# Quantised ffn of a two-layer decoder: GpSimd adds two tiles back ahead of the row quantisation, TensorE and ScalarE in another order, six unread 512-column products a tile

## The chip, the core and the metric

The kernel runs on one NeuronCore of a Trainium2 chip, in one launch. The metric is the device time of the launch in microseconds (us). The core has five engines that run their own instruction lists and meet at semaphores: TensorE (PE, matrix products into PSUM), VectorE (DVE), ScalarE (ACT), GpSimd (POOL, SBUF only) and SyncE (SP, here the DMA queue). Each takes its instructions strictly in order; an instruction whose semaphore isn't there yet holds up all that stand behind it on the same engine.

## The reference

A pre-norm decoder of two layers on x of 64 x 64 rows of 256 numbers: attention, cross attention and an ffn, each added to x, twice. Only the last ffn is touched. It quantises its inputs, its weights and its hidden rows to whole numbers from -127 to 127 with one scale a row:

```python
def _quant_dequant(v, axis):
    scale = jnp.max(jnp.abs(v), axis=axis, keepdims=True) / QMAX   # QMAX = 127
    scale = jnp.maximum(scale, EPS)
    q = jnp.clip(jnp.round(v / scale), -QMAX, QMAX)
    return q * scale

xq = _ste(x, axis=-1)                    # x: the layer-normed rows, 256 wide
gate_up = jnp.einsum('bsh,oh->bso', xq, _ste(w_gate_up, axis=-1))
gate, up = (gate_up[..., :I], gate_up[..., I:])          # I = 704
h = jax.nn.silu(gate) * up
return jnp.einsum('bsi,oi->bso', _ste(h, axis=-1), _ste(w_down, axis=-1))
# and the decoder: x = x + _L1_ffn_ref(_layernorm(x), ...)
```

`_ste(v)` is the quantised v in value.

## The kernel before

The 4,096 rows are 32 tiles of 128 rows and lie in SBUF the whole time (`x_all`). The stage of interest is `ffn_quantised`, the last one. The weights are quantised once ahead of it (`quantise_weights`), as whole numbers in bf16, which TensorE multiplies exactly; the scales are multiplied in behind it. For tile t the work is:

- VectorE: mean and variance of the rows (`stats`, f_ and ln_ names in the profile: ln_st, ln_mv).
- GpSimd: `ln.pool_step` makes 1/sqrt(var + eps) (`ln_ve`, `ln_rstd`), `mean_shift` makes minus mean times that (`minus_mean`, `shift`).
- ScalarE: `normalise` writes the normed rows (`ln_xn`). VectorE: `scale_x` takes the largest absolute value of a row, its scale and the reciprocal (`stat`).
- GpSimd: `x_quantised` multiplies by the reciprocal (`xm`), adds a large constant, which rounds (`xr`), and takes it away again (`xq`, bf16).
- TensorE: `x_transpose` (2 transposes), ScalarE: `x_transposed` copies to `xt`. TensorE: `gate_and_up`, 8 products of 352 columns.
- VectorE: `gate` and `up` out of PSUM with both scales; ScalarE: Silu (`sig`); VectorE: `make_h`, the product `h`, its largest value, scale and reciprocal (`hstat`).
- ScalarE: `h_quantised` (`hr`, `hq`). TensorE: `transpose_h`, 6 transposes, ScalarE: `h_transposed` copies to `ht`. TensorE: `down`, 6 products of 256 columns into one of two PSUM banks (6 and 7, by the parity p of the tile).
- ScalarE: `y_scaled` (`yt`), GpSimd: `add`, times the weights' scale (`ys`) and onto `x_all`. SyncE stores two tiles at a time once they are added.

The order on each engine is written out by hand: `over_tiles` calls `step(t, p, has_next)` for each tile, first and last pair unrolled, the others in a hardware loop of two tiles. A step holds pieces of several tiles: in step t GpSimd prepares x of t+2 and then adds t-1; ScalarE does Silu of t, xt of t+1, ht of t-1, normalises t+2, quantises h of t and scales y of t-1; TensorE transposes h of t-1, makes gate and up of t+1, down of t-1 and transposes x of t+2; VectorE does the statistics of t+2, gate, up and h of t and the scale of x of t+2. `wait_used(engine, semaphore, t, buffers)` waits until a buffer's earlier tile has been read. `started(t)` is false for the first tile, `further(t)` for the last two.

Of the kernel before, what the change touches and what calls it, by code (L numbers as in the profile page):

```python
# [25 lines left out]
TILES = 32  # L26
# [2347 lines left out]

FF = 704
QMAX, Q_EPS = 127.0, 1e-8
ROUND = 1.5 * 2.0 ** 23


def ffn_quantised(m, stage):  # L2380
# [11 lines left out]
    with ExitStack() as ctx:  # L2392
# [35 lines left out]
        ht_ps = ps[:, 5, 0:C2 * P // 2].bitcast(BF16)  # L2428
        y_ps = lambda p: ps[:, 6 + p, 0:DM]
        halves = lambda a: a.rearrange("p (k n) -> p k n", k=2)  # L2430
        started = lambda t: not (isinstance(t, int) and t < 1)
        further = lambda t: not (isinstance(t, int) and t + 2 >= TILES)
        hmul_ready, xm_ready, ys_ready = sem("hmul_ready"), sem("xm_ready"), sem("ys_ready")
        rnd_set, xs_ready, xr_ready, hs_ready, hr_ready = (sem(n) for n in ("rnd_set", "xs_ready", "xr_ready", "hs_ready", "hr_ready"))
# [21 lines left out]
        @block.gpsimd  # L2456
        def _(pool):
            def mean_shift(t, p):

                wait_used(pool, shift_ready, t, 1)  # L2460
                pool.tensor_tensor(minus_mean[:, :], ln.mv[:, p, 0:1], minus[:, :], ALU.mult).then_inc(minus_ready, 1)
                pool.wait_ge(minus_ready, t + 1)
                pool.wait_ge(ln.rstd_ready, t + 1)
                wait_used(pool, ln.xn_ready, t, 2)
                pool.tensor_tensor(shift[:, p], minus_mean[:, :], ln.rstd[:, p], ALU.mult).then_inc(shift_ready, 1)

            def x_quantised(t, p):

                wide = lambda a: a.to_broadcast([P, DM])
                pool.wait_ge(xs_ready, t + 1)  # L2470
                wait_used(pool, xr_ready, t, 1)
                pool.tensor_tensor(xm[:, :], ln.xn[:, p], wide(stat[:, p, 2:3]), ALU.mult).then_inc(xm_ready, 1)  # L2472
                pool.wait_ge(xm_ready, t + 1)
                wait_used(pool, xq_ready, t, 1)
                pool.tensor_tensor(xr[:, :], xm[:, :], wide(rnd[:, 0]), ALU.add).then_inc(xr_ready, 1)  # L2475
                pool.wait_ge(xr_ready, t + 1)
                wait_used(pool, xtp_ready, t, 2)
                pool.tensor_tensor(xq[:, p], xr[:, :], wide(rnd[:, 1]), ALU.add).then_inc(xq_ready, 1)  # L2478

            def add(t, p):  # L2480
                pool.wait_ge(yt_ready, t + 1)
                wait_used(pool, x_done, t, 1)
                pool.tensor_tensor(ys[:, :], yt[:, p], s2[:, :], ALU.mult).then_inc(ys_ready, 1)  # L2483
                pool.wait_ge(ys_ready, t + 1)
                x = m.x_all[:, at(t), :]
                ys_ = ys[:, :] if isinstance(t, int) else ys[:, :].rearrange("p (a n) -> p a n", a=1)
                pool.tensor_tensor(x, x, ys_, ALU.add).then_inc(x_done, 1)

            def head():
                pool.memset(minus[:, :], -1.0).then_inc(minus_set, 1)  # L2490
                ln.pool(pool)
                pool.wait_ge(minus_set, 1)
                mean_shift(0, 0)
                ln.pool_step(pool, 1, 1)
                mean_shift(1, 1)
                pool.wait_ge(rnd_set, 2)
                x_quantised(0, 0)
                x_quantised(1, 1)

            def step(t, p, has_next):  # L2500
                if further(t):
                    ln.pool_step(pool, t + 2, p)
                    mean_shift(t + 2, p)
                    x_quantised(t + 2, p)
                if started(t):
                    add(t - 1, 1 - p)
            over_tiles(pool, head, step)
            add(TILES - 1, 1)

        @block.scalar  # L2510
        def _(act):
            def x_transposed(t, p):
                act.wait_ge(xtp_ready, t + 1)
                wait_used(act, gu_ready, t, 2)
                act.copy(xt[:, p].rearrange("p c s -> p (c s)"), xt_ps).then_inc(xt_ready, 1)

            def h_transposed(t):
                act.wait_ge(htp_ready, t + 1)
                wait_used(act, y_ready, t, 1)
                act.copy(ht[:, :, :].rearrange("p c s -> p (c s)"), ht_ps).then_inc(ht_ready, 1)  # L2520

            def normalise(t, p):

                act.wait_ge(shift_ready, t + 1)
                wait_used(act, xm_ready, t, 2)
                act.activation(ln.xn[:, p], m.x_all[:, at(t), :], ACT.Identity, scale=ln.rstd[:, p],
                               bias=shift[:, p]).then_inc(ln.xn_ready, 1)

            def y_scaled(t, p):
                act.wait_ge(y_ready, t + 1)  # L2530
                wait_used(act, ys_ready, t, 2)
                act.activation(yt[:, p], y_ps(p), ACT.Copy, scale=hstat[:, p, 1:2]).then_inc(yt_ready, 1)  # L2532

            def h_quantised(t, p):
                act.wait_ge(hs_ready, t + 1)
                act.activation(hr[:, :], h[:, :], ACT.Identity, scale=hstat[:, p, 2:3], bias=rnd[:, 0]).then_inc(hr_ready, 1)  # L2536
                act.wait_ge(hr_ready, t + 1)
                wait_used(act, htp_ready, t, 2)
                act.activation(hq[:, p, 0:FF], hr[:, :], ACT.Identity, bias=rnd[:, 1]).then_inc(hq_ready, 1)  # L2539

            def head():
                act.wait_ge(rnd_set, 2)
                normalise(0, 0)
                normalise(1, 1)
                x_transposed(0, 0)

            def step(t, p, has_next):
                act.wait_ge(gate_ready, t + 1)
                wait_used(act, hmul_ready, t, 1)
                act.activation(sig[:, :], gate[:, :], ACT.Silu).then_inc(sig_ready, 1)  # L2550
                if has_next:
                    x_transposed(t + 1, 1 - p)
                if started(t):
                    h_transposed(t - 1)
                if further(t):
                    normalise(t + 2, p)
                h_quantised(t, p)
                if started(t):
                    y_scaled(t - 1, 1 - p)
            over_tiles(act, head, step)  # L2560
            h_transposed(TILES - 1)
            y_scaled(TILES - 1, 1)
# [47 lines left out]
        @block.tensor  # L2610
        def _(pe):
            def x_transpose(t, p):
                pe.wait_ge(xq_ready, t + 1)
                wait_used(pe, xt_ready, t, 1)
                for c in range(KC):
                    last = pe.transpose(xt_ps[:, c * P:(c + 1) * P], xq[:, p, c * P:(c + 1) * P], m.identb[:, :])
                last.then_inc(xtp_ready, 1)

            def gate_and_up(t, p):
                pe.wait_ge(xt_ready, t + 1)  # L2620
                wait_used(pe, up_ready, t, 1)
                for c in range(KC):
                    for k in range(4):
                        last = pe.matmul(ps[:, 1 + k, 0:HF], xt[:, p, c, :], w1[:, c, k * HF:(k + 1) * HF],  # L2624
                                         start=c == 0, stop=c == KC - 1)
                last.then_inc(gu_ready, 1)

            def transpose_h(t, p):
                pe.wait_ge(hq_ready, t + 1)
                wait_used(pe, ht_ready, t, 1)  # L2630
                for c in range(C2):
                    last = pe.transpose(ht_ps[:, c * P:(c + 1) * P], hq[:, p, c * P:(c + 1) * P], m.identb[:, :])  # L2632
                last.then_inc(htp_ready, 1)

            def down(t, p):
                pe.wait_ge(ht_ready, t + 1)
                wait_used(pe, yt_ready, t, 2)
                for c in range(C2):
                    k = P if c < C2 - 1 else tail
                    last = pe.matmul(y_ps(p), ht[0:k, c, :], w2[0:k, c, :], start=c == 0, stop=c == C2 - 1)  # L2640
                last.then_inc(y_ready, 1)

            def head():
                x_transpose(0, 0)
                gate_and_up(0, 0)
                x_transpose(1, 1)

            def step(t, p, has_next):
                if started(t):
                    transpose_h(t - 1, 1 - p)  # L2650
                if has_next:
                    gate_and_up(t + 1, 1 - p)
                if started(t):
                    down(t - 1, 1 - p)
                if further(t):
                    x_transpose(t + 2, p)
            over_tiles(pe, head, step)
            transpose_h(TILES - 1, 1)
            down(TILES - 1, 1)
# [198 lines left out]
```

## Time and profile before

| | us |
|---|---|
| median of 3 runs | 3217.69 (3211.05 to 3225.68) |
| profiled execution, its own time | 3207.37 |
| its span in the trace | 3205.5 |
| busy: TensorE, VectorE, ScalarE, GpSimd | 2644.7, 2030.2, 1581.7, 1372.7 |
| last stage, from 3040 to 3120: the same four | 51.12, 59.82, 52.53, 54.56 |
| granted TensorE clock, whole span and 3040 to 3120 | 0.943 and 0.65 |

The span covers all stages. The quantised ffn begins at about 2968 us, when VectorE starts on the statistics of its first tile, and ends with the span. Busy time is summed over instructions; for TensorE it is modelled, as products overlap, and it stretches where the granted clock is lower. The granted clock is a share of 2.4 GHz: 1.00 is 2.4 GHz and 0.50 is 1.2 GHz, and a mean between them is a mix of stretches at the two.

### The profile page before, as it was taken

What the parts mean: (1) busy time and instruction counts of PE and PEld (TensorE: products, weight loads), DVE (VectorE), ACT (ScalarE), POOL (GpSimd) and SP (SyncE); (2) the same over time, 40 slices, a digit from 0 to 9 for tenths busy, and PEclk for the clock granted to TensorE, in tenths of its full rate; (3) what the DMA queues carried; (4) which work ended last, traced back from release to release, by engine and by line L of the source; (5) the groups of instructions that cost most, each with busy time, mean ns of one, the idle gap of its engine ahead of it and who ended that gap; (6) DMA issues with size and microseconds to landing.
All of it is one profiled execution on the core that took longest, in us unless ns stands there. A gap on an engine that the chain in (4) does not pass through costs nothing. (4 is left out here: it accounts for less than half of the span.)

```text
span 3205.5 us, 85997 instructions
## 1 busy us (share of the span) xinstructions
PE 2644.7 (83%) x33006; PEld 1936.5 (60%) x33006; DVE 2030.2 (63%) x3706; ACT 1581.7 (49%) x2950; POOL 1372.7 (43%) x1490
## 2 busy tenths in 40 slices
PE   3888888888858888867677779999999999997565
PEld 2677777777732222224466667888788888886333
DVE  6888888888858888848577743434343434334776
ACT  3555555555527777731334313443434444443566
POOL 4888888888822333224222212222222212221665
PEclk9999999999969999979799989999999999999667
DMA  3000000000013333300100020000000000000000
GB/s 120 2 0 0 0 0 0 0 0 0 0 49 89 89 90 90 92 13 0 31 24 25 26 69 6 7 6 7 6 7 6 7 6 7 5 33 1 13 16 23
DMA packets 94784, 77.50 MB, mean 24 GB/s; under 512 B 17520, under 2 KB 88560, under 8 KB 93424
## 3 DMA queue, kind: packets, MB, share of 16 engines
q1 hardware_dynamic: 94576, 74.35, 7.6%
q8 instruction: 177, 2.90, 0.4%
q14 instruction: 31, 0.25, 0.0%
HBM read 55.97 MB, written 17.04 MB: 23 GB/s over the span
## 5 line engine op out<-in xcount | busy, mean ns | idle before, releaser
L1394 DVE TENSOR_REDUCE x_mx<-x_ps 128x2 f16<-128x512 f32 x512 | 330.8, 682 | 47.0 <-PE x_ps L1458 44.5
L1363 ACT ACTIVATE x_e<-x_ps 128x512 f32<-128x512 f32 x512 | 291.9, 596 | 46.2 <-PE x_ps L1462 30.2
L361 POOL TENSOR_TENSOR x1s<-x1s,x1mx 128x1024 f32<-128x1024 f32 x32 | 60.9, 1902 | 542.3 <-DVE x1mx L357 542.3
L1722 ACT ACTIVATE x_q<-x_ps,x_q_bias,x_q_scale 128x128 f32<-128x128 f32 x512 | 186.1, 467 | 162.0 <-PE x_ps L105 161.9
L1458 PE MATMUL x_ps<-x_k,x_q 32*128 32x256 f16 x1024 | 194.7, 281 | 82.4 <-ACT x_e L1363 53.1
L431 ACT CAST x1oh<-x_ps 128x1024 f16<-128x1024 f32 x64 | 64.7, 1012 | 328.9 <-PE x_ps L423 328.9
L103 PE MATMUL a_ps<-ln_xha,a_wq 128*128 128x128 f16 x1024 | 181.0, 222 | 51.3 <-ACT a0v L678 43.8
L1458 PEld LDWEIGHTS x_ps<-x_k,x_q 32*128 32x128 f16 x1024 | 58.7, 92 | 261.6 <-DVE x_mx L1394 126.2
L627 POOL TENSOR_TENSOR a_w<-a_qsw,a_tab 128x512 f32<-128x512 f32 x128 | 176.8, 1381 | 58.1 <-ACT a_qsw L688 56.7
L1462 PE MATMUL x_ps<-x_q,x_k 32*128 32x256 f16 x1024 | 196.5, 283 | 1.7 <-ACT x_e L1363 1.4
L280 DVE TENSOR_TENSOR ln_xlx<-x_ps,ln_xhx 128x256 f16<-128x256 f32 x32 | 13.6, 424 | 289.0 <-ACT x_xt L1714 289.0
L105 PE MATMUL x_ps<-x_chi,x_w 128*128 128x128 f16 x1024 | 180.9, 221 | 16.2 <-issue 16.2
L103 PE MATMUL x_ps<-x_chi,x_w 128*128 128x128 f16 x1024 | 181.5, 221 | 1.7 <-DVE x_z L1800 1.7
L769 DVE TENSOR_TENSOR a_u<-a_u,a_w 128x512 f32<-128x512 f32 x128 | 181.9, 1441 | 0.0
L104 PE MATMUL x_ps<-x_clo,x_w 128*128 128x128 f16 x1024 | 180.8, 220 | 0.0
L104 PE MATMUL a_ps<-ln_xla,a_wq 128*128 128x128 f16 x1024 | 180.2, 221 | 0.0
L105 PE MATMUL a_ps<-ln_xha,a_wq 128*128 128x128 f16 x1024 | 180.2, 221 | 0.0
L103 PE MATMUL x_ps<-ln_xhx,x_w 128*128 128x128 f16 x1024 | 178.6, 221 | 0.0
L104 PE MATMUL x_ps<-ln_xlx,x_w 128*128 128x128 f16 x1024 | 178.6, 221 | 0.0
L105 PE MATMUL x_ps<-ln_xhx,x_w 128*128 128x128 f16 x1024 | 178.5, 221 | 0.0
L632 POOL TENSOR_TENSOR a_sql<-a_sq,a_sqh 128x512 bf16<-128x512 f32 x128 | 176.3, 1377 | 0.0
L1495 PE MATMUL x_ps<-x_e,x_vt 128*9 128x256 f32 x2048 | 166.5, 399 | 0.1
(365 smaller groups left out, 9120.4 us busy)
## 6 DMA issues: line engine op xcount, KB each, us to landing
x_q<-x_q_rows SPq DMA_DIRECT2D x32, 256.0 KB, 2.8
x_k<-x_k_rows SPq DMA_DIRECT2D x32, 256.0 KB, 3.1
a_stage<-in_x_w SPq DMA_DIRECT2D x32, 256.0 KB, 2.6
x_vt<-in_ctx_v SPq DMA_DIRECT2D x32, 144.0 KB, 2.3
stage<-in_x_wt SPq DMA_DIRECT2D x4, 1028.0 KB, 6.4
x_all<-in_x SPq DMA_DIRECT2D x8, 512.0 KB, 9.9
x_cf<-in_ctx SPq DMA_DIRECT2D x32, 128.0 KB, 2.1
x_q_rows<-x_xhl SPq DMA_DIRECT2D x32, 128.0 KB, 1.7
```

Source lines behind the costliest of these rows:

```text
L103: pe.matmul(out, a[0], b[0], start=start, stop=False)
L104: pe.matmul(out, a[0], b[1], start=False, stop=False)
L105: return pe.matmul(out, a[1], b[0], start=False, stop=stop)
L627: pool.tensor_tensor(by_head(w, g), by_head(qsw, g), table(QW), ALU.mult).then_inc(w_ready, 1)
L632: pool.tensor_tensor(by_head(sql, g), by_head(sq, g), by_head(sqh, g), ALU.subtract).then_inc(sql_ready, 1)
L769: dve.tensor_tensor(by_head(u, g), by_head(u, g), by_head(w, g), ALU.add).then_inc(uw_ready, 1)
L1363: act.activation(e[:, u % ES].rearrange("p c n -> p (c n)"), s2_ps(u), ACT.Exp, scale=XT ** -0.5).then_inc(e_ready, 1)
L1394: dve.reduce_max(mx[:, p % 2, c:c + 2], s1_ps(u), AX).then_inc(mx_ready, 1)
L1458: return pe.matmul(s1_ps(u)[:, c], q[r, p % 4, g, c * P:(c + 1) * P], k[r, p % 4, g], start=True, stop=True)
L1462: return pe.matmul(s2_ps(u)[:, c * DM:(c + 1) * DM], k[r, p % 4, g, c * P:(c + 1) * P], q[r, p % 4, g], start=True, stop=True)
L1495: last = pe.matmul(o_ps[32 * jj:32 * jj + VC, g % 2, :], vt[:, p % 2, n, u, :], e[:, u % ES, n, :], start=n == 0, stop=n == KC - 1)
L1722: last = act.activation(q[:, i, :], ps[:, bank(4 + g), h * P:(h + 1) * P], ACT.Identity, scale=q_scale[:, i:i + 1], bias=q_bias[:, i:i + 1])
```

## The change

GpSimd's step now adds tile t-2, and does so between the small instructions for x of t+2 and its quantisation. ScalarE copies ht ahead of xt, and scales y of t-1 ahead of quantising h of t. TensorE transposes x of t+1 behind the transposes of h, makes down ahead of gate and up, and gets six products a tile of 512 columns, three ahead of down and three at the step's end. Their result goes to the y bank (6 or 7) whose next content the down products start afresh, and nothing reads it. All that is computed is as before.

```diff
+BUSY = 3
-        started = lambda t: not (isinstance(t, int) and t < 1)
+        started = lambda t, lag: not (isinstance(t, int) and t < lag)
@@ gpsimd
                 if further(t):
                     ln.pool_step(pool, t + 2, p)
                     mean_shift(t + 2, p)
+                if started(t, 2):
+                    add(t - 2, p)
+                if further(t):
                     x_quantised(t + 2, p)
-                if started(t):
-                    add(t - 1, 1 - p)
             over_tiles(pool, head, step)
+            add(TILES - 2, 0)
             add(TILES - 1, 1)
@@ scalar
                 act.activation(sig[:, :], gate[:, :], ACT.Silu).then_inc(sig_ready, 1)
+                if started(t, 1):
+                    h_transposed(t - 1)
                 if has_next:
                     x_transposed(t + 1, 1 - p)
-                if started(t):
-                    h_transposed(t - 1)
                 if further(t):
                     normalise(t + 2, p)
+                if started(t, 1):
+                    y_scaled(t - 1, 1 - p)
                 h_quantised(t, p)
-                if started(t):
-                    y_scaled(t - 1, 1 - p)
@@ tensor
+            def keep_busy(t, p):
+
+                wait_used(pe, yt_ready, t, 2)
+                for _ in range(BUSY):
+                    pe.matmul(ps[:, 6 + p, :], m.identb[:, :], w1[:, 0, 0:512], start=True, stop=True)
+
             def head():
                 x_transpose(0, 0)
                 gate_and_up(0, 0)
-                x_transpose(1, 1)
             def step(t, p, has_next):
-                if started(t):
+                if started(t, 1):
                     transpose_h(t - 1, 1 - p)
                 if has_next:
+                    x_transpose(t + 1, 1 - p)
+                if started(t, 1):
+                    keep_busy(t - 1, 1 - p)
+                    down(t - 1, 1 - p)
+                if has_next:
                     gate_and_up(t + 1, 1 - p)
-                if started(t):
-                    down(t - 1, 1 - p)
-                if further(t):
-                    x_transpose(t + 2, p)
+                keep_busy(t, p)
```

GpSimd's list in the second tile of the loop, before. The four small ones and xm, xr, xq belong to tile t+2, ys and x_all to t-1.

```order
L250 TENSOR_TENSOR ln_vef<-ln_mvf,ln_epsf 128x1
L252 TENSOR_TENSOR ln_rstdf<-ln_vef,mhalf 128x1
L2461 TENSOR_TENSOR f_minus_mean<-ln_mvf,f_minus 128x1
L2465 TENSOR_TENSOR f_shift<-f_minus_mean,ln_rstdf 128x1
L2472 TENSOR_TENSOR f_xm<-ln_xnf,f_stat 128x256
L2475 TENSOR_TENSOR f_xr<-f_xm,f_rnd 128x256
L2478 TENSOR_TENSOR f_xq<-f_xr,f_rnd 128x256
L2483 TENSOR_TENSOR f_ys<-f_yt,f_s 128x256
L2487 ISA
L2487 TENSOR_TENSOR x_all<-x_all,f_ys 128x256
```

The same place now; ys and x_all are those of t-2.

```order
L250 TENSOR_TENSOR ln_vef<-ln_mvf,ln_epsf 128x1
L252 TENSOR_TENSOR ln_rstdf<-ln_vef,mhalf 128x1
L2462 TENSOR_TENSOR f_minus_mean<-ln_mvf,f_minus 128x1
L2466 TENSOR_TENSOR f_shift<-f_minus_mean,ln_rstdf 128x1
L2484 TENSOR_TENSOR f_ys<-f_yt,f_s 128x256
L2488 ISA
L2488 TENSOR_TENSOR x_all<-x_all,f_ys 128x256
L2473 TENSOR_TENSOR f_xm<-ln_xnf,f_stat 128x256
L2476 TENSOR_TENSOR f_xr<-f_xm,f_rnd 128x256
L2479 TENSOR_TENSOR f_xq<-f_xr,f_rnd 128x256
```

The adding back has moved from behind xq to between the shift and xm.

TensorE's list in the second tile of the loop, before: transposes of h (t-1), gate and up (t+1), down (t-1), transposes of x (t+2).

```order
L2632 MATMUL f_ps<-identb,f_hq 128x128 x6
L2624 MATMUL f_ps<-f_w,f_xt 128x352 x8
L2640 MATMUL f_ps<-f_w,f_ht 128x256 x6
L2613 REGISTER_ALU
L2616 MATMUL f_ps<-identb,f_xq 128x128 x2
```

The same place now: the transposes of x are those of t+1, and L2650 are the products that nothing reads.

```order
L2635 MATMUL f_ps<-identb,f_hq 128x128 x6
L2616 REGISTER_ALU
L2619 MATMUL f_ps<-identb,f_xq 128x128 x2
L2650 MATMUL f_ps<-f_w,identb 128x512 x3
L2643 MATMUL f_ps<-f_w,f_ht 128x256 x6
L2627 MATMUL f_ps<-f_w,f_xt 128x352 x8
L2650 MATMUL f_ps<-f_w,identb 128x512 x3
```

The transposes of x moved by one step and lie between those of h and down, down and gate and up have changed places, and the new products stand ahead of the two waits, for ht and for the next hq.

ScalarE's list there now, from Silu of t on: f_ht and f_yt of t-1, f_xt of t+1, the normalisation of t+2, f_hr and f_hq of t.

```order
L2553 ACTIVATE f_sig<-f_gate 128x704
L2523 COPY f_ht<-f_ps 128x768
L2518 COPY f_xt<-f_ps 128x256
L2527 REGISTER_ALU
L2529 ISA
L2529 ACTIVATE ln_xnf<-x_all,f_shift,ln_rstdf 128x256
L2535 ACTIVATE f_yt<-f_ps,f_hstat 128x256
L2539 ACTIVATE f_hr<-f_h,f_rnd,f_hstat 128x704
L2542 ACTIVATE f_hq<-f_hr,f_rnd 128x704
```

Before, f_xt stood ahead of f_ht, and f_yt behind f_hq.

## Rows read from the trace of the kernel before

**Rows 1.** Stretches: us, busy (instructions) of PE, PEld, DVE, ACT, POOL, clock, DMA, GB/s.
```profile
1440.00:1520.00 80.00, 58.01 (x428) 33.46 (x428) 67.81 (x285) 15.33 (x48) 34.72 (x71) 1.00 0.00 0
...
3040.00:3120.00 80.00, 51.12 (x262) 28.22 (x260) 59.82 (x136) 52.53 (x80) 54.56 (x105) 0.65 0.06 20
```

**Rows 2.** Who waited for whom, 2980 to 3206: us, times, longest.
```profile
PE f_ps L2616 <- POOL f_xq L2478: 73.1, 30, 4.0
POOL f_xm L2472 <- DVE f_stat L2571: 53.1, 30, 5.2
...
DVE ln_stf L255 <- issue: 3.4, 13, 0.3
```

**Rows 3.** Timeline of GpSimd: start, us, instruction, [idle before <-releaser].
```profile
3065.45 0.61 POOL L2472 TENSOR_TENSOR f_xm<-ln_xnf,f_stat 128x256 f32<-128x256 f32 x1 [1.64 <-DVE f_stat L2571]
...
3067.41 0.73 POOL L2483 TENSOR_TENSOR f_ys<-f_yt,f_s 128x256 f32<-128x256 f32 x1
3068.40 1.07 POOL L2487 TENSOR_TENSOR x_all<-x_all,f_ys 128x256 f32 x1 [0.27 <-POOL f_ys L2483]
...
3070.48 0.19 POOL L2465 TENSOR_TENSOR f_shift<-f_minus_mean,ln_rstdf 128x1 f32<-128x1 f32 x1
3072.32 0.61 POOL L2472 TENSOR_TENSOR f_xm<-ln_xnf,f_stat 128x256 f32<-128x256 f32 x1 [1.64 <-DVE f_stat L2571]
```

**Rows 4.** Timeline of VectorE, the same tile.
```profile
3065.21 0.16 DVE L2571 RECIPROCAL f_stat<-f_stat 128x1 f32<-128x1 f32 x1
...
3067.76 1.12 DVE L2582 TENSOR_TENSOR f_h<-f_up,f_sig 128x704 f32<-128x704 f32 x1
...
3071.43 0.42 DVE L2569 TENSOR_REDUCE f_stat<-ln_xnf 128x1 f32<-128x256 f32 x1 [1.24 <-ACT ln_xnf L2526]
...
3072.07 0.16 DVE L2571 RECIPROCAL f_stat<-f_stat 128x1 f32<-128x1 f32 x1
```

**Rows 5.** Timeline of VectorE, second and third tile of the stage.
```profile
2983.15 0.16 DVE L2571 RECIPROCAL f_stat<-f_stat 128x1 f32<-128x1 f32 x1
...
2985.64 0.91 DVE L2582 TENSOR_TENSOR f_h<-f_up,f_sig 128x704 f32<-128x704 f32 x1
...
2988.49 0.16 DVE L2571 RECIPROCAL f_stat<-f_stat 128x1 f32<-128x1 f32 x1
...
2991.44 0.89 DVE L2582 TENSOR_TENSOR f_h<-f_up,f_sig 128x704 f32<-128x704 f32 x1 [0.32 <-ACT f_sig L2550]
```

**Rows 6.** Timeline of GpSimd, the second tile.
```profile
2985.62 0.55 POOL L252 TENSOR_TENSOR ln_rstdf<-ln_vef,mhalf 128x1 f32<-128x1 f32 x1
2986.14 0.46 POOL L2461 TENSOR_TENSOR f_minus_mean<-ln_mvf,f_minus 128x1 f32<-128x1 f32 x1
```

**Rows 7.** Timeline of all engines, tile 30.
```profile
3185.53 0.89 DVE L2582 TENSOR_TENSOR f_h<-f_up,f_sig 128x704 f32<-128x704 f32 x1 [0.19 <-ACT f_sig L2550]
3185.55 1.45 POOL L2483 TENSOR_TENSOR f_ys<-f_yt,f_s 128x256 f32<-128x256 f32 x1
```

**Rows 8.** Timeline of TensorE, gate and up at either clock.
```profile
3061.60 2.55 PE L2624 MATMUL f_ps<-f_w,f_xt 128*128 128x352 bf16 x8
...
3068.26 1.37 PE L2624 MATMUL f_ps<-f_w,f_xt 128*128 128x352 bf16 x8
```

**Rows 9.** TensorE's groups from 1440 to 1520: xcount, busy us, mean ns.
```profile
L103 PE MATMUL f_ps<-f_wb,ln_xhf 128*128 128x256 f16 x47 | 12.8, 273 | 0.0
...
L105 PE MATMUL f_ps<-f_wa,ln_xlf 128*128 128x136 f16 x48 | 9.6, 223 | 0.0
...
L105 PE MATMUL f_ps<-f_wB,f_hl 128*128 128x256 f16 x24 | 6.5, 273 | 0.0
```

**Rows 10.** Timeline of all engines, the end of the last tile.
```profile
3193.30 0.97 ACT L2536 ACTIVATE f_hr<-f_h,f_rnd,f_hstat 128x704 f32<-128x704 f32 x1 [1.58 <-DVE f_hstat L2571]
...
3196.64 1.57 PE L2640 MATMUL f_ps<-f_w,f_ht 128*128 128x256 bf16 x6 [0.89 <-ACT f_ht L2520]
...
3198.25 0.47 ACT L2532 ACTIVATE f_yt<-f_ps,f_hstat 128x256 f32<-128x256 f32 x1 [1.67 <-PE f_ps L2640]
```

## The prediction

> **What bounds the kernel now.** I read the stretches first, then who waits for whom in the last stage, then one tile engine by engine. The quantised ffn fills the last 235 us, one tile after another. Its stretch from 3040 to 3120 us has no engine near its limit: VectorE is busy 59.8 us of 80, GpSimd 54.6, ScalarE 52.5, TensorE 51.1, and TensorE's granted clock is 0.65 [rows 1]. From the product of tile 2 at 2991.44 us to that of tile 30 at 3185.53 us are 28 tiles in 194.1 us, 6.93 us each [rows 5, 7]. So 80 us hold 11.5 tiles, and ScalarE works 4.55 us on each, VectorE 5.2.
>
> The waits show a ring [rows 2]: TensorE waits for xq of GpSimd (73.1 us in 30 times), and GpSimd for the row scale of VectorE (53.1 us); VectorE in turn waits for ScalarE's normalised rows [rows 4]. In one tile [rows 3]: xm at 3065.45, ys at 3067.41, x_all at 3068.40, shift at 3070.48, and then GpSimd is idle 1.64 us, while ScalarE normalises and VectorE takes the scale (its reduction at 3071.43 after 1.24 us idle, the reciprocal at 3072.07) [rows 4]; xm follows at 3072.32. All nine GpSimd instructions, the normalisation and the scale stand in this ring in series: 6.87 us here, and that is the tile time. The adding back (ys and x_all, 3067.41 to 3069.47, 2.1 us) is in the ring though nothing in the ring needs it.
>
> **GpSimd's order.** The add goes between the shift and xm, and takes tile t-2, whose yt ScalarE has made a step earlier, so it shouldn't wait. It now lies beside the normalisation and the scale. The ring that is left: reciprocal to xm 0.25 (3072.07 to 3072.32), xm to the end of xq 1.96 (65.45 to 67.41), the statistics' four small ones to the shift's start 1.01 (69.47, where x_all ends, to 70.48), shift to reduction 0.95, reduction to reciprocal 0.64: 4.8 us [rows 3, 4]. GpSimd by itself: 6.87 less its wait of 1.64, 5.2 us. So neither bounds any more; VectorE does.
>
> **VectorE's own time.** Reciprocal to reciprocal is 3065.21 to 3072.07, 6.86 us; without the idle 1.24 that is 5.62. The product f_h took 1.12 there, where 0.91 and 0.89 are the other tiles' [rows 4, 5]; less these 0.2, 5.4. Every second tile has some 0.26 us before its statistics (3.4 us in 13 times) [rows 2], 0.1 on the mean: 5.5 us. The trace has one tile that ran that way, the second, which has nothing to add: reciprocal at 2983.15, the next at 2988.49, 5.34 us [rows 5]. It did so with TensorE at the lower clock.
>
> **The port between VectorE and GpSimd.** Where f_h began at 3185.53, ys of GpSimd, from 3185.55, took 1.45 us and not 0.73 [rows 7]; so GpSimd waits while f_h runs. With the add moved f_h, 2.5 us after the reciprocal (2983.15 to 2985.64), meets the small instructions instead. The second tile shows this too: rstd at 2985.62, minus_mean at 2986.14 took 0.46 [rows 6], 0.27 over the 0.19 of shift, which is of its size [rows 3]. Worst, a small one starts just behind f_h and waits all its 0.9 us: the ring becomes 4.8 to 5.7 us, 5.1 with the 0.27. Neither is much over VectorE's 5.5. From below, f_h escapes the 1.12 and no wait is added: 5.4. From above, f_h waits for rstd, 0.55 long, or parts of both waits add up: 6.1. I take 5.65, near to the one tile that shows it and a little above, since ring, VectorE and GpSimd lie within 0.5 us and will not always mesh.
>
> The Trainium skill (SBUF — State Buffer, the section "SBUF: two separate sides") says of this port pair that whichever starts first has it for the whole instruction and the other fully blocks, for a VectorE operation with two SBUF inputs against a reading GpSimd one. The row of ys agrees. The rows of the second tile do not agree to the letter: f_h began 0.02 us behind rstd and took 0.91, no 0.5 longer [rows 5, 6]. By the rule to the letter 0.5 us a tile would come on top, 28 x 0.5 = 14 us less gained; by the row nothing.
>
> **ScalarE's order.** y_scaled of t-1 now stands ahead of h_quantised of t, so hr waits for the down products. The new ring is hr, hq, transposes, ht, down, yt, hr. The tail has it without anything in between: hr starts at 3193.30, yt ends at 3198.72 [rows 10], 5.4 us with down at the lower clock (1.57 us). At the full clock down takes about half, which makes 4.7 us. Silu of t+1 precedes ht in the order, but is done by then in most tiles: about 1 us of room under 5.65. At the lower clock there is none (below).
>
> **TensorE.** Before, a tile has 8 x 128 + 8 x 352 + 6 x 256 = 5,376 columns. The two groups of three products add 3,072, 8,448 in all. The 2,816 columns of gate and up take 1.37 us at the full and 2.55 us at half the clock [rows 8], so a tile costs 8,448 / 2,816 = 3 times that: 4.1 us at full, 7.65 at half. The clock decides whether they are free. At full they fit: 1.5 us lie where TensorE waits (transposes of x at one end, hq at the other), and 1.5 us remain. They write only the y bank that the down products overwrite, and the wait ahead of them is the one that down has, met a step earlier. Queued behind them are the down products, which wait for ht anyhow (three products, about 0.75 us at the full clock, while ScalarE makes it), and the transposes of h.
>
> What says that the clock is full: the first layer's ffn, from 1440 to 1520 us, has 1.00 throughout with TensorE busy 58.0 of 80 us [rows 1]. Its columns there, three lines of each of three forms, are 3 x (47 x 256 + 48 x 136 + 24 x 256) = 74,112 [rows 9]; at 2.4 GHz 30.9 us, 39% of the stretch, its own transposes not counted. The changed tile has 7,424 without its transposes, 3.1 us of 5.65: 55%, with busy 4.1 of 5.65, 73%, like that stage (72.5%). Before it is 4,352 columns, 1.8 us of 6.93: 26%. Its idle pieces, 73.1 / 30 = 2.4 us each before the transposes of x [rows 2], shrink to about 1.
>
> **The sum.** 28 tiles x (6.93 - 5.65) = 35.8 us saved. The first tiles run at the lower clock with the added columns: up to two tiles x (7.65 - 5.5), of which I take 3 us lost. The tail keeps its chain; one more add stands in it, but beside TensorE's work. The gain is 33 us. The profiled execution, 3207.4 us with a span of 3205.5, becomes 3174. Its time is 10 us below the median shown (3217.7, runs from 3211 to 3226), and the saving is the same, so the forecast is 3185 us.
>
> **Rivals.**
> 1. TensorE stays at 1.2 GHz in the stage (slower). It is then the bound with 7.65 us a tile, and its unread products are the price: 28 x 0.72 = 20 us, and 3 at the start: 3241. It decides once the full clock is granted for less than about an eighth of the time (the mean of the two speeds then gives 6.93). For: 0.65 now, with idle and busy stretches in turns [rows 1]. Against: at the half clock TensorE would be busy without a pause, and the first stages hold the clock with less. 8%.
> 2. The clock keeps falling and rising. Half the time at each level makes TensorE's tile 5.3 us, but in a slow stretch it and ScalarE's new ring (down at the lower clock, the three products ahead of it) give 7 or more; about 6.6 on the mean, 9 us saved, 3 lost: 3212. 12%. The Trainium skill has a rule for this (TensorE: Matmul & The Clock Gate, the section "A second HAM failure mode: psum-queue depth-cycling"): many small idle pieces between groups of matmuls can be enough for the clock to swing. The rows from 1440 to 1520 us, with TensorE idle 27% in small pieces and a clock of 1.00, speak against it.
> 3. The port and the meshing cost more than I take, f_h and GpSimd's instructions pushing each other every tile: 6.4 us, 15 saved, 3 lost: 3206. For it is GpSimd's want of room (5.2 and the waits behind f_h). 8%.
> 4. That the add is not off the ring, because yt of t-2 is late, I give nothing of its own: in the tile of rows 3 even yt of t-1 is there when ys comes up 1.96 us after xm, and t-2 is a whole tile older.
>
> **How the numbers follow.** The forecast has 72%. Its own range is 5.4 to 6.1 us a tile: 43 to 23 saved, 3 lost, 3178 to 3198. About 0.5%, 16 us, is what a measurement here can tell from none. Under 3201.6 lie the forecast and a little of rivals 2 and 3: 0.74 faster; slower by over 0.5% is rival 1, 0.08; the rest 0.18. The range for 8 in 10 is 3172 to 3212: the forecast's with some us for the spread between runs at its low end, and up to rival 2; outside lie rival 1, half of rival 2 and little at the low end.
>
> **What would show it.** Right: the stage's clock at 0.95 or more; f_h to f_h 5.5 to 5.8 us; no idle on VectorE before the reduction of x, GpSimd's wait before xm down from 1.64 to under 0.5 us; the waits of TensorE for xq gone, those for hq or ht in their place; minus_mean or shift stretched beside f_h. Wrong: matmuls of gate and up still at 2.5 us; gate and up of VectorE waiting for TensorE; ScalarE's hr waiting for yt with VectorE's reciprocal long past; ys waiting for yt. The prediction falls if the clock is under 0.9, or if a tile takes over 6.1 us at the full one.

## The result: 1.35% faster, at VectorE's own time a tile

The changed kernel takes 3173.0 us (median of 4 runs, 3168.3 to 3182.4) against 3217.1 (4 runs, 3211.1 to 3225.7): a ratio of 0.9865, 95% interval 0.9833 to 0.9897. The forecast was 3185, range 3172 to 3212, so the result lies 1 us inside the range's low end. The profiled executions differ by 35.1 us of span (3205.5 and 3170.4). Where it lies, by the product f_h, which comes once a tile on VectorE (columns as before: start, us, instruction):

```profile
2985.68 0.89 DVE L2585 TENSOR_TENSOR f_h<-f_up,f_sig 128x704 f32<-128x704 f32 x1
...
2997.19 1.43 DVE L2585 TENSOR_TENSOR f_h<-f_up,f_sig 128x704 f32<-128x704 f32 x1
...
3150.82 0.91 DVE L2585 TENSOR_TENSOR f_h<-f_up,f_sig 128x704 f32<-128x704 f32 x1
```

From tile 2 to tile 30 it is 153.6 us where it was 194.1 [rows 5, 7]: 5.49 us a tile and not 6.93, 40.5 us less. Tile 0 comes 5.3 us later (2985.68, before 2980.41), in stages whose code is the same; over the fourteen kernels profiled here, with this pair, that start lies anywhere from 2978 to 2997. The first two tiles lost 0.5 us, the tail gained 0.4: 40.5 - 5.3 - 0.5 + 0.4 = 35.1. So times of whole runs carry some 10 us that aren't this stage's, and below a tile's time is read from f_h of tile 2 to f_h of tile 30, over 28.

The f_h of tile 2 took 1.43 us and not 0.89. GpSimd's ys had begun 0.04 us ahead of it (below, at the port):

```profile
2997.15 0.72 POOL L2484 TENSOR_TENSOR f_ys<-f_yt,f_s 128x256 f32<-128x256 f32 x1
```

Stretches of the changed kernel (us; PE, PEld, DVE, ACT, POOL busy; clock; DMA):

```profile
1440.00:1520.00 80.00, 58.05 (x429) 33.59 (x429) 67.81 (x286) 15.30 (x48) 34.53 (x71) 1.00 0.00 0
...
3040.00:3120.00 80.00, 62.24 (x409) 31.33 (x409) 73.81 (x172) 64.67 (x102) 69.85 (x133) 1.00 0.08 26
```

Against [rows 1]: VectorE from 59.8 to 73.8 of 80, GpSimd to 69.9, and TensorE's clock from 0.65 to 1.00. TensorE's 62.2 us over 14.6 tiles are 4.3 us each, the prediction's 4.1.

Who waited for whom, 2980 us to the end:

```profile
PE f_ps L2635 <- ACT f_hq L2542: 25.6, 32, 2.0
...
PE f_ps L2619 <- POOL f_xq L2479: 20.7, 30, 10.0
...
ACT ln_xnf L2529 <- POOL f_shift L2466: 14.9, 28, 0.6
...
POOL f_xm L2473 <- DVE f_stat L2574: 11.6, 17, 5.2
...
DVE ln_stf L255 <- issue: 3.4, 13, 0.3
```

The 73.1 and 53.1 us of [rows 2] are 20.7 and 11.6 (10.0 and 5.2 of these are single waits at the start of the stage), and VectorE waits for nothing in the loop but its own 0.26 us of issue (idle time for which the profile shows no releaser, once in two tiles). One tile of VectorE, and of GpSimd, which answer to [rows 4] and [rows 3]:

```profile
3044.51 0.17 DVE L2574 RECIPROCAL f_stat<-f_stat 128x1 f32<-128x1 f32 x1
...
3045.19 0.92 DVE L2604 SCALAR_TENSOR_TENSOR f_gate<-f_ps,f_stat,f_s 128x704 f32<-128x704 f32 x1
...
3047.06 0.89 DVE L2585 TENSOR_TENSOR f_h<-f_up,f_sig 128x704 f32<-128x704 f32 x1
...
3049.19 0.42 DVE L2572 TENSOR_REDUCE f_stat<-ln_xnf 128x1 f32<-128x256 f32 x1
...
3049.83 0.16 DVE L2574 RECIPROCAL f_stat<-f_stat 128x1 f32<-128x1 f32 x1
3050.25 0.43 DVE L255 BATCH_NORM_STATS2 ln_stf<-x_all 128x6 f32 x1 [0.26 <-issue]
```

```profile
3044.75 0.61 POOL L2473 TENSOR_TENSOR f_xm<-ln_xnf,f_stat 128x256 f32<-128x256 f32 x1
...
3046.97 0.55 POOL L252 TENSOR_TENSOR ln_rstdf<-ln_vef,mhalf 128x1 f32<-128x1 f32 x1
3047.48 0.52 POOL L2462 TENSOR_TENSOR f_minus_mean<-ln_mvf,f_minus 128x1 f32<-128x1 f32 x1
3048.08 0.19 POOL L2466 TENSOR_TENSOR f_shift<-f_minus_mean,ln_rstdf 128x1 f32<-128x1 f32 x1
3048.22 0.73 POOL L2484 TENSOR_TENSOR f_ys<-f_yt,f_s 128x256 f32<-128x256 f32 x1
3049.14 0.73 POOL L2488 TENSOR_TENSOR x_all<-x_all,f_ys 128x256 f32 x1 [0.19 <-POOL f_ys L2484]
3050.08 0.61 POOL L2473 TENSOR_TENSOR f_xm<-ln_xnf,f_stat 128x256 f32<-128x256 f32 x1 [0.21 <-DVE f_stat L2574]
```

The reduction has no idle time before it, and reciprocal to reciprocal is 5.32 us; with the pause at the loop's turn the next tile is 5.66. The adding lies at 3048.22 to 3049.87, beside VectorE's scale of h and x. GpSimd waits 0.21 us in one tile of two.

### The profile page after: what moved, and what is told of

Its sections match the earlier page's. It is cut to its first block and busy times, and to the rows that moved or that the text cites. A ratio compares the mean times of both kernels' runs of the same rounds, so it can differ in the third digit from the quotient of the medians.

```text
span 3170.4 us, 86390 instructions
## 1 busy us (share of the span) xinstructions
PE 2651.1 (84%) x33195; PEld 1929.0 (61%) x33195; DVE 2026.1 (64%) x3706; ACT 1576.7 (50%) x2950; POOL 1372.2 (43%) x1490
## 5 line engine op out<-in xcount | busy, mean ns | idle before, releaser
L769 DVE TENSOR_TENSOR a_u<-a_u,a_w 128x512 f32<-128x512 f32 x128 | 181.7, 1440 | 0.0
```

The lines of the kernel that those rows point to most:

```text
L769: dve.tensor_tensor(by_head(u, g), by_head(u, g), by_head(w, g), ALU.add).then_inc(uw_ready, 1)
```

## The experiments

The tile times and clocks, each from its own profile (clock from 3040 to 3120 us, f_h of tiles 2 and 30). Each ratio is to executions of the kernel before taken with that run:

| kernel | clock | f_h, tile 2 and 30 | us a tile | median us | ratio to before |
|---|---|---|---|---|---|
| before | 0.65 | 2991.44, 3185.53 | 6.93 | 3217.1 | |
| changed | 1.00 | 2997.19, 3150.82 | 5.49 | 3173.0 | 0.987 (0.983 to 0.990) |
| GpSimd's order alone | 0.81 | 3000.98, 3155.18 | 5.51 | 3176.4 | 0.986 (0.982 to 0.990) |
| changed, no unread products | 0.67 | 3009.14, 3185.99 | 6.32 | 3199.2 | 0.993 (0.991 to 0.996) |
| changed, GpSimd's old order | 0.88 | 2995.19, 3188.45 | 6.90 | 3215.6 | 1.000 (0.998 to 1.002) |
| changed, 2 unread products | 0.89 | 2991.17, 3150.34 | 5.68 | 3172.2 | 0.986 (0.982 to 0.990) |
| changed, 12 | 1.00 | 2992.50, 3146.01 | 5.48 | 3168.9 | 0.988 (0.985 to 0.991) |
| changed, 18 | 1.00 | 2997.09, 3176.01 | 6.39 | 3199.9 | 0.995 (0.993 to 0.997) |
| GpSimd's order, 3 products | 0.88 | 3000.22, 3153.89 | 5.49 | 3180.0 | 0.990 (0.986 to 0.993) |
| GpSimd's order, unrolled by 4 | 0.85 | 2995.54, 3148.12 | 5.45 | 3169.9 | 0.987 (0.984 to 0.990) |
| GpSimd's and TensorE's order, ScalarE's ht ahead of xt | 0.67 | 2990.29, 3165.52 | 6.26 | 3193.6 | 0.994 (0.991 to 0.997) |
| GpSimd's and ScalarE's order | 0.63 | 2996.60, 3223.36 | 8.10 | 3249.2 | 1.011 (1.006 to 1.016) |
| changed, no up pass | 1.00 | 2997.94, 3150.14 | 5.44 | 3172.1 | 0.987 (0.985 to 0.990) |
| the same, no wait for Silu | 1.00 | 2992.58, 3129.66 | 4.90 | 3149.6 | 0.980 (0.975 to 0.984) |

**GpSimd's order alone.** The rival to my theory was that TensorE's clock plays no part at all.

```diff
 # before.py, shortened; TensorE and ScalarE untouched
                     mean_shift(t + 2, p)
-                    x_quantised(t + 2, p)
-                if started(t):
-                    add(t - 1, 1 - p)
+                if started(t, 2):
+                    add(t - 2, p)
+                if further(t):
+                    x_quantised(t + 2, p)
...
+            add(TILES - 2, 0)
```

> The kernel before with GpSimd's new order alone (add of t-2 between the shift and xm); TensorE and ScalarE as before, no unread products. Theory A (the shorter ring gives the gain, but only with the full clock): TensorE's clock stays at about 0.65 in the stage, its slow tiles hold up gate and up, a tile takes 5.9 to 6.3 us, and the kernel is 18 to 28 us faster than before. Rival R (the clock plays no part at this size, 5,376 columns are 4.9 us at half the clock): 5.5 us a tile as in the changed kernel, 38 to 44 us faster, with the clock still low.

Measured: 5.51 us a tile, 3176.4 us. The rival holds on the time; its clock was to stay low, and it is 0.81, where the theory had 0.65. TensorE's timeline shows a tile at half the clock fitting in (start, us, instruction, [idle before]):

```profile
3044.52 0.28 PE L2618 MATMUL f_ps<-identb,f_xq 128*128 128x128 bf16 x2 [0.99 <-POOL f_xq L2478]
...
3050.17 0.39 PE L2618 MATMUL f_ps<-identb,f_xq 128*128 128x128 bf16 x2 [2.64 <-POOL f_xq L2478]
3050.36 0.85 PE L2634 MATMUL f_ps<-identb,f_hq 128*128 128x128 bf16 x6
3051.03 2.41 PE L2626 MATMUL f_ps<-f_w,f_xt 128*128 128x352 bf16 x8
3053.27 0.92 PE L2642 MATMUL f_ps<-f_w,f_ht 128*128 128x256 bf16 x6
3055.51 0.29 PE L2618 MATMUL f_ps<-identb,f_xq 128*128 128x128 bf16 x2 [1.31 <-POOL f_xq L2478]
```

Gate and up took 2.41 us there, and TensorE still idled 1.31 before the next transposes of x. In 16 of the 32 tiles gate and up took 2.28 us or more, and VectorE never waits for them in the loop. The lower level reached it once all the same: down took 1.60 us from 3081.06, ScalarE's yt waited 0.50 us for it ahead of Silu, and f_h at 3083.96 waited 0.49 us for Silu. No run kept the clock at its lower level in every tile.

**All orders, no unread products.**

```diff
-BUSY = 3
+BUSY = 0
```

> The changed kernel with BUSY = 0: all three orders, none of the unread products. Theory A: the clock falls to 0.7 or so; with down ahead of gate and up, and yt ahead of hq, a tile at the half clock takes over 6.3 us (reciprocal to xq 2.2, transposes 0.4, down 1.6 behind ht, gate and up 2.4, which reach VectorE over 1 us late every second tile), the mean 6.0 to 6.3: 15 to 25 us slower than the changed kernel. Rival R: 5.5 us a tile, the same time as the changed kernel.

Measured: clock 0.67, 6.32 us, 3199.2. The theory holds, just past its edge. TensorE, and VectorE in the same stretch:

```profile
3047.11 0.39 PE L2619 MATMUL f_ps<-identb,f_xq 128*128 128x128 bf16 x2
3048.29 1.55 PE L2643 MATMUL f_ps<-f_w,f_ht 128*128 128x256 bf16 x6 [0.79 <-ACT f_ht L2523]
3049.77 2.53 PE L2627 MATMUL f_ps<-f_w,f_xt 128*128 128x352 bf16 x8
```

```profile
3050.41 0.17 DVE L2574 RECIPROCAL f_stat<-f_stat 128x1 f32<-128x1 f32 x1
...
3052.34 0.95 DVE L2604 SCALAR_TENSOR_TENSOR f_gate<-f_ps,f_stat,f_s 128x704 f32<-128x704 f32 x1 [1.16 <-PE f_ps L2627]
```

Gate and up stand behind down, which waits for ht. They end at 3052.30, and VectorE waits 1.16 us for them. From 3010 to 3180 us it waits for them 19 times, 15.7 us in all; the loss against GpSimd's order alone is 28 x 0.81 = 22.7 us.

**GpSimd's old order, all else changed.**

```diff
 # after.py, shortened
-                if started(t, 2):
-                    add(t - 2, p)
-                if further(t):
-                    x_quantised(t + 2, p)
+                    x_quantised(t + 2, p)
+                if started(t, 1):
+                    add(t - 1, 1 - p)
```

> The changed kernel with GpSimd's order of before (quantise x of t+2, then add t-1); TensorE's and ScalarE's new orders and the six unread products stay. Theory A: the ring through all nine GpSimd instructions is back, 6.8 to 6.95 us a tile whatever the clock (0.95 or more), within 8 us of the kernel before. Rival R2 (the gain comes from the clock and TensorE's order): at least half the gain stays, over 20 us faster than before.

Measured: 6.90 us, ratio 1.000. The ring is back with GpSimd's wait, and the clock of 0.88 (expected 0.95 or more) buys nothing:

```profile
3040.75 0.61 POOL L2473 TENSOR_TENSOR f_xm<-ln_xnf,f_stat 128x256 f32<-128x256 f32 x1 [1.64 <-DVE f_stat L2572]
...
3047.61 0.61 POOL L2473 TENSOR_TENSOR f_xm<-ln_xnf,f_stat 128x256 f32<-128x256 f32 x1 [1.64 <-DVE f_stat L2572]
```

**Two unread products.** `BUSY = 1`.

> The changed kernel with BUSY = 1, two unread products a tile instead of six: 5,376 + 1,024 = 6,400 columns. Theory A: at 5.5 us a tile, 5,376 counted columns without transposes are 2.2 us, 41%, about what the first layer's ffn has (39%), so the clock holds or nearly: 0.9 or more and within 6 us of the changed kernel. Rival: it is too few, the clock is at 0.7 to 0.8 and the kernel 8 to 20 us slower than the changed one.

Measured: 0.89, just under the theory's 0.9, and 5.68 us a tile. Two products don't quite hold the clock; by the tiles that costs 28 x 0.20 = 5.5 us, which the whole time (3172.2) doesn't show. From 3005 to 3150 us VectorE waits 4.7 us for gate and up, in 9 times. Within the theory's 6 us.

**Twelve.** `BUSY = 6`.

> The changed kernel with BUSY = 6, twelve unread products a tile: 11,520 columns, at 1.37 us for 2,816 of them 5.6 us of TensorE a tile, more than VectorE's 5.5, and three more products stand ahead of down. Theory A: TensorE is the bound, a tile takes 5.7 to 6.3 us at the full clock, 6 to 22 us slower than the changed kernel. Rival: the products lie where TensorE waits in any number, the time is the changed kernel's within 4 us.

Measured: 5.48 us. The theory failed and the rival holds. TensorE is busy 75.8 of 80 us and still waits. That is 75.8 / 14.6 = 5.2 us a tile and not my 5.6. I had scaled the 1.37 us of gate and up, but a group's shown time overlaps with the next one's: here the next group starts 1.20 us after it.

```profile
3060.21 1.37 PE L2627 MATMUL f_ps<-f_w,f_xt 128*128 128x352 bf16 x8
3061.41 1.46 PE L2650 MATMUL f_ps<-f_w,identb 128*128 128x512 bf16 x6
```

At 1.20 us for 2,816 columns the 11,520 are an estimated 4.9 us a tile.

**Eighteen.** `BUSY = 9`.

> The changed kernel with BUSY = 9, eighteen unread products a tile: 14,592 columns. By the last stage's busy time with twelve (75.8 of 80 us, 5.2 us a tile at 5.50) six more at 0.21 us each make 6.5 us of TensorE a tile. Theory E (TensorE is free up to VectorE's 5.5 us and the bound beyond): 6.2 to 6.6 us a tile, 20 to 30 us slower than the changed kernel. Rival (TensorE's products never hold up a tile, whatever their number): the changed kernel's time.

Measured: 6.39 us, 3199.9: TensorE is busy 80.0 of 80 us and is the bound. So the free room ends between 12 and 18. The theory holds.

**GpSimd's order with three products in the old orders.**

```diff
 # on GpSimd's order alone, TensorE's step
                     down(t - 1, 1 - p)
+                keep_busy(t, p)          # three products
                 if further(t):
                     x_transpose(t + 2, p)
```

> GpSimd's new order alone (as in the first experiment) with TensorE's and ScalarE's old orders, and three unread products of 512 columns a tile ahead of the transposes of x, where TensorE waits some 2 us for xq. Theory C (with the old orders the clock is worth nothing, since a tile at the half clock fits into VectorE's 5.5 us): the clock rises from 0.81 to 0.9 or more, the tile stays at 5.50 us, time within 4 us of the first experiment's. Rival (clock still worth something): over 5 us faster, or, where the products delay the transposes of x, the tile goes to 5.7 us or more.

Measured: clock 0.88 after 0.81, 5.49 us a tile after 5.51. With the old orders a higher clock brings nothing that can be told (3180.0 and 3176.4 us). The clock was expected at 0.9.

**Unrolled by four.**

```diff
 # on GpSimd's order alone, all four engines
-            over_tiles(pe, head, step)
+            over_tiles(pe, head, lambda t, p, n: step(t, p % 2, n), 4)
```

> GpSimd's new order alone, and the loops of this stage unrolled over four tiles instead of two, no unread products. Theory C: VectorE alone sets the pace and its pause at each turn of the loop (0.26 us before the statistics, tiles of 5.66 and 5.33 us in turns) comes half as often: mean tile 5.42 us instead of 5.50, some 2 us less, too little to be told by the time. Rival: GpSimd's room of 0.2 us is gone, the tile stays at 5.50.

Measured: 5.45 us from tile 2 to 30; f_h comes after 5.77, 5.47, 5.33 and 5.33 us in turns, 5.475 on the mean in the loop. The pause comes half as often but is longer (0.36 us before the statistics and not 0.26). That lies between the theory's 5.42 and the rival's 5.50, and no gain can be told.

**Which of the two orders needs the clock.** First TensorE's order without ScalarE's yt in front:

```diff
 # after.py with BUSY = 0, ScalarE's step; h_transposed stays ahead of x_transposed
-                if started(t, 1):
-                    y_scaled(t - 1, 1 - p)
                 h_quantised(t, p)
+                if started(t, 1):
+                    y_scaled(t - 1, 1 - p)
```

> The changed kernel without unread products, and yt of t-1 behind hq of t on ScalarE as it was before; GpSimd's new order and TensorE's new order stay. It asks which of the two orders lost time without the full clock. Theory D (TensorE's order: gate and up behind down reach VectorE late at the half clock): a tile takes 6.0 to 6.4 us, as with all orders and no unread products (6.32), some 25 us slower than GpSimd's order alone. Rival (ScalarE's yt ahead of hq did it): 5.5 to 5.7 us a tile.

Measured: 6.26 us, against 6.32 with ScalarE's too. So it isn't yt ahead of hq; it is TensorE's order, as the theory has it, or TensorE's order together with ht ahead of xt on ScalarE, which this kernel keeps and no run took away. The whole time is 17 us over that of GpSimd's order alone, by the tiles 28 x 0.75 = 21. Then ScalarE's new order with TensorE's old one:

```diff
 # GpSimd's order alone, ScalarE's step
+                if started(t):
+                    h_transposed(t - 1)
                 if has_next:
                     x_transposed(t + 1, 1 - p)
-                if started(t):
-                    h_transposed(t - 1)
                 if further(t):
                     normalise(t + 2, p)
+                if started(t):
+                    y_scaled(t - 1, 1 - p)
                 h_quantised(t, p)
-                if started(t):
-                    y_scaled(t - 1, 1 - p)
```

> GpSimd's new order and ScalarE's new order, TensorE's order of before, no unread products. ScalarE then waits for ht before xt, and for down, which stands behind gate and up, before hq: the ring hq, transposes 0.6, ht 0.8, xt 0.35, gate and up 1.2, down 0.9, yt 0.45, hr and hq 1.9 is 6.3 us at the full and over 8 at the half clock. Theory D (the two orders belong together): 6.5 to 7.5 us a tile, 28 to 55 us slower than GpSimd's order alone. Rival (ScalarE's order is harmless): within 5 us of it.

Measured: 8.10 us, 3249.2: slower than before the change. The direction was right, the size short (6.5 to 7.5 expected). The clock fell to 0.63, and in most tiles gate and up take 2.53 us, where the expectation has the ring at over 8 us. ScalarE in that kernel:

```profile
3050.59 0.47 ACT L2534 ACTIVATE f_yt<-f_ps,f_hstat 128x256 f32<-128x256 f32 x1 [3.66 <-PE f_ps L2642]
3050.96 0.96 ACT L2538 ACTIVATE f_hr<-f_h,f_rnd,f_hstat 128x704 f32<-128x704 f32 x1
```

**VectorE without its pass for up.** What stands next behind VectorE?

```diff
 # after.py, VectorE; the waits that go with it left out here
-                dve.tensor_tensor(h[:, :], up[:, :], sig[:, :], ALU.mult).then_inc(hmul_ready, 1)
+                dve.scalar_tensor_tensor(halves(h[:, :]), up_ps, stat[:, p, 1:2], halves(sig[:, :]),
+                                         ALU.mult, ALU.mult).then_inc(hmul_ready, 1)
...
-                dve.scalar_tensor_tensor(halves(up[:, :]), up_ps, stat[:, p, 1:2], halves(s1[:, FF:]),
-                                         ALU.mult, ALU.mult).then_inc(up_ready, 1)
```

> The changed kernel with VectorE's pass for up left out: h is made in one pass from up in PSUM, the row scale and Silu, and the column scale of up is left out of the computation. VectorE's tile falls from 5.5 to about 4.6 us, and f_h has one SBUF input only. Theory B (GpSimd is right behind VectorE): the tile becomes GpSimd's own 4.75 us (no waits behind f_h are left: xm to xq's end 1.96, small ones 1.04, ys to x_all 0.92, x_all 0.83) or the ring's 4.8, so 4.75 to 4.95 us, and minus_mean is back at 0.19 us. Rival (the waits of GpSimd beside f_h have another cause than f_h's second SBUF input): minus_mean stays at 0.5 to 0.85 us and the tile is 5.2 us or more.

Measured: 5.44 us a tile. The theory failed on time, and so did its rival on the cause:

```profile
3050.77 0.95 DVE L2604 SCALAR_TENSOR_TENSOR f_gate<-f_ps,f_stat,f_s 128x704 f32<-128x704 f32 x1
3052.57 0.95 DVE L2584 SCALAR_TENSOR_TENSOR f_h<-f_ps,f_stat,f_sig 128x704 f32<-128x704 f32 x1 [0.86 <-ACT f_sig L2553]
```

```profile
3052.76 0.19 POOL L2462 TENSOR_TENSOR f_minus_mean<-ln_mvf,f_minus 128x1 f32<-128x1 f32 x1
```

minus_mean beside f_h is back at 0.19 us, so f_h's second SBUF input was what held it up. But VectorE now idles 0.86 us for Silu: from the start of gate to that of f_h it is 1.80 us (3050.77 to 3052.57) by way of Silu, and was 1.87 us (3045.19 to 3047.06) by way of up. To show that, f_h was made from gate and not from Silu of gate:

```diff
 # against the kernel just above; the waits that go with it left out here
-                dve.scalar_tensor_tensor(halves(h[:, :]), up_ps, stat[:, p, 1:2], halves(sig[:, :]),
+                dve.scalar_tensor_tensor(halves(h[:, :]), up_ps, stat[:, p, 1:2], halves(gate[:, :]),
                                          ALU.mult, ALU.mult).then_inc(hmul_ready, 1)
```

> As the kernel without VectorE's pass for up, but h is made from gate and not from Silu of gate, so VectorE doesn't wait for ScalarE between them (the column scale of up and Silu's place in h are left out of the computation; ScalarE still makes Silu). Theory F (with up gone VectorE waited 0.86 us for Silu; up lies in that wait, so the chain gate, Silu, h is as long as gate, up, h): the tile falls from 5.46 to 4.7 to 4.95 us, where GpSimd or the ring of normalisation and quantisation bounds. Rival (another bound lies at 5.46, GpSimd's or ScalarE's ring): 5.3 us or more.

Measured: 4.90 us, as expected, 3149.6 us of whole time. GpSimd now runs without a wait before xm, so its own list is the bound:

```profile
3039.86 0.61 POOL L2473 TENSOR_TENSOR f_xm<-ln_xnf,f_stat 128x256 f32<-128x256 f32 x1
...
3044.82 0.61 POOL L2473 TENSOR_TENSOR f_xm<-ln_xnf,f_stat 128x256 f32<-128x256 f32 x1
```

## Why the prediction was right, and where it was off

- **The ring through GpSimd bounds, and the adding in it is what costs.** Right, and shown from both sides: GpSimd's order alone gives 5.51 us a tile, everything but it 6.90.
- **VectorE bounds next, at 5.5.** Right: 5.49, with the 5.34 of the second tile [rows 5] as 5.32 to 5.34 in every other tile. I put 5.65 for want of room between three chains. That margin, 28 x 0.16 = 4.5 us, is the term that was mis-sized, and the 3 us for the first tiles were 0.5. With the tail's 0.4 they are the 7.4 us between 33 forecast and 40.4 measured in this stage. The rest of the distance to the medians' 44 lies outside this stage. For the profiled execution 3174 was forecast and 3172.3 measured, and that this is so near is luck: the stage gained 7.4 us more than forecast, and its start, where nothing was changed, came 5.3 us later.
- **What "VectorE's own time" is.** The term's name was incomplete. Without the pass for up VectorE is busy 62.3 of 80 us and not 73.8, 0.83 us a tile less, and the tile gave 0.05; gate, Silu and f_h are a chain over two engines of the same length. Only with Silu's wait gone too did the tile fall, to 4.90.
- **The port.** Right in size, 0.5 to 0.85 us on minus_mean and none of it in the tile time: the ring has room for it. The rule of the Trainium skill (SBUF — State Buffer, "SBUF: two separate sides"), read to the letter, has f_h wait for rstd. In the loop rstd runs from 3046.97 to 3047.52 and f_h, begun at 3047.06, takes its 0.89; in the 28 tiles where rstd is under way it takes 0.89 or 0.90. Here the measurement decides: a 128x1 rstd does not hold up f_h (as far as the profile times GpSimd's instructions). In the other direction the rule holds: minus_mean, begun behind f_h, waits for it. And it holds for a full-width GpSimd instruction ahead of f_h: in tile 2 of the changed kernel ys began at 2997.15, and f_h, from 2997.19, took 1.43 us. The 1.12 us of [rows 4] are the same: ys began 0.35 us ahead there [rows 3]. The new order has ys behind f_h, and f_h is back at 0.89, the 0.2 us that the prediction took off.
- **TensorE's clock.** The forecast of 1.00 was right (rivals 1 and 2 didn't come), and TensorE becomes the bound between twelve and eighteen products. How far the comparison with the first layer's ffn carries is open: for two unread products it gave 0.9 or more, and 0.89 came. But I let the clock decide over the gain, and for the change as a whole that is wrong: the gain is there at 0.81 with half the tiles at the lower level, and it is TensorE's new order (with ht ahead of xt) that needs the full clock. Without unread products the clock was 0.67 and the tile 6.32. Of the six products' work 5.49 against 6.32 is real, yet it repairs what the order ahead of it had cost (5.51 to 6.26). That VectorE waits for gate and up accounts for 15.7 of the 22.7 us lost without the products; that down at the half clock behind ht is what makes them late was read from one tile, not taken apart, and the 7.65 us a tile of rival 1 had no run of its own.
- **ScalarE's order.** Its yt ahead of hq is harmless with TensorE's new order (6.26 and 6.32); both its moves with the old one are ruinous (8.10). Its ht ahead of xt had no run alone. The prediction had the ring but only priced it for the pair.
- **The tail.** I took down's 1.57 us [rows 10] to shrink at the full clock. It is 1.57 again; the clock is at 0.50 in that moment in the changed kernel too, where TensorE has little left to do.

## What to carry to other kernels

When a ring through several engines is as long as a tile, look in it for work that the ring doesn't need, and put it where its engine waits for the others; that alone was the gain here, and an early tile of the old trace that lacked the work had shown the new tile time. Try each part of a change by itself: here GpSimd's order gave everything, the orders of TensorE and ScalarE cost 0.8 us a tile and the unread products paid that back. The version with GpSimd's order alone takes the same time with no unread products. An engine busy 92% of the time may still hide a chain over two engines just as long, so taking work off it can bring nothing.

## What was unexpected of the hardware

- Unread products are free up to nearly a full TensorE: with twelve a tile it is busy 75.8 of 80 us and no tile is longer; eighteen make it 80.0 and 0.9 us a tile.
- Busy time doesn't rank the clocks: with GpSimd's order alone the clock is 0.81 with TensorE busy 53.2 of 80 us, with all orders and no unread products 0.67 with 56.3. Busy time stretches where the clock is lower, and the second kernel made 12.7 tiles in those 80 us and the first 14.5. Whether the order of the work plays a part of its own in the clock, no run here shows.
- GpSimd's 128x1 rstd under way doesn't hold up VectorE's f_h (0.89 or 0.90 us in 28 tiles), a 128x256 ys does (1.43 and 1.12 us), and a 128x1 minus_mean that starts behind f_h waits for its end (0.52 and 0.85 us in place of 0.19).
